# Per-image products of the diffuser as six pairs of heads on four column or row groups

## The reference

```python
k = (ref @ k_w).reshape(NB_REF, N, HEADS, hd).transpose(0, 2, 1, 3)
for _ in range(STEPS):                                    # 3
    qv = (x @ qv_w).reshape(B, N, 2, HEADS, hd).transpose(2, 0, 3, 1, 4)
    q, v = (qv[0], qv[1])
    attn = jnp.einsum('bhnd,rhmd->brhnm', q, k) * scale   # 12 heads of 16
    attn = jnp.einsum('brhnm,brhkm->brhnk', attn, attn)
    o = jnp.einsum('brhnk,bhkd->brhnd', attn, v)
    o = o.reshape(B, NB_REF, N, C)    # head-major, without a transpose back
    x = jnp.mean(o.transpose(0, 2, 3, 1), axis=-1)
    x = _layernorm(x @ proj_w + proj_b, ln_g, ln_b)
```

## Time and profile before

| | |
|---|---|
| median of three runs | 565.02 us (564.35 to 565.89) |
| the profiled execution | 566.11 us, its span 564.3 us |
| mean granted clock of TensorE | 0.804 of 2.4 GHz |
| busy: PE, PEld, DVE, ACT, POOL | 442.6, 365.1, 295.7, 244.8, 209.2 us |

### The profile page before, as it was taken

One profiled execution on the slowest core, in us unless ns is written; L12 is line 12 of the kernel. 1 busy time (PEld: TensorE's weight loads), 2 busy tenths in 40 slices (PEclk: granted clock), 3 DMA queues, 4 the chain that ended last, 5 costly groups with the idle time before them and its releaser, 6 DMA issues.

```text
span 564.3 us, 12817 instructions
## 1 busy us (share of the span) xinstructions
PE 442.6 (78%) x4112; PEld 365.1 (65%) x4112; DVE 295.7 (52%) x914; ACT 244.8 (43%) x724; POOL 209.2 (37%) x318
## 2 busy tenths in 40 slices
PE   3992699799999973789999997731989898989800
PEld 3972567587888752779998986631866666666600
DVE  0110423255555668687789775455545454545456
ACT  0130235566666641477656763111544444444300
POOL 1000004355455558353656552453232323232233
PEclk9996579799999975576767675555799999999955
DMA  8709525364455530000000000012111111100041
GB/s 263 202 23 322 163 46 122 77 161 94 100 116 117 112 82 0 1 2 2 2 2 14 25 14 14 18 47 90 51 37 33 32 34 36 32 15 19 6 145 44
DMA packets 52031, 38.32 MB, mean 68 GB/s; under 512 B 36059, under 2 KB 45445, under 8 KB 51200
## 3 DMA queue, kind: packets, MB, share of 16 engines
q1 hardware_dynamic: 48704, 26.78, 18.9%
q10 hardware_dynamic: 1008, 7.15, 3.9%
q0 software_dynamic: 2256, 3.57, 2.0%
HBM read 23.89 MB, written 14.33 MB: 68 GB/s over the span
## 4 chain that ended last, share of the span: by engine, by line
PE 68%; DVE 9%; issue 7%; POOL 4%; DMA 4%; ACT 3%; ACTq 3%; SPq 1%; POOLq 0%; DVEq 0%
PE bank L337 61%; PE bank L342 3%; PE bank L509 3%; ACTq L648 2%; ACT xT L738 2%; DVE h L1118 2%; POOL srt_dram L1174 1%; DMA bdm<-in_bdm 1%; PE bank L585 1%; DVE stats L815 1%; POOL rstd L1147 1%; DMA xT<-in_w 1%; SPq L274 1%; DVE xT L823 0%; ACT xT L633 0%
## 5 line engine op out<-in xcount | busy, mean ns | idle before, releaser
L337 PE MATMUL bank<-xh,w1h 96*128 96x128 f16 x300 | 69.6, 233 | 13.1 <-issue 11.9
L337 PE MATMUL bank<-xT 108*108 108x17 f16 (+5 forms) x904 | 67.9, 255 | 15.2 <-ACT xT L633 10.9
L337 PE MATMUL bank<-xl,w1h 96*128 96x128 bf16 x300 | 67.3, 225 | 0.0
L337 PE MATMUL bank<-xh,w1l 96*128 96x128 f16 x300 | 67.1, 224 | 0.0
L337 PEld LDWEIGHTS bank<-xT 108*108 108x108 bf16 (+4 forms) x904 | 50.9, 162 | 22.8 <-ACT xT L633 11.0
L791 ACT ACTIVATE xT<-bank,b 128x128 f32<-128x128 f32 x150 | 47.0, 364 | 41.3 <-PE bank L337 41.0
L633 ACT ACTIVATE xT<-bank 108x192 f32<-108x192 f32 (+3 forms) x117 | 40.1, 397 | 55.4 <-PE bank L337 37.5
L1217 POOL DMA_INDIRECT y_dram<-qkbm,ydst x25 | 24.8, 991 | 96.5 <-DVE qkbm L1109 87.5
L337 PEld LDWEIGHTS bank<-xh,w1h 96*128 x300 | 29.7, 99 | 32.8 <-issue 19.3
L666 ACT ACTIVATE xT<-bank,gains 96x128 f32<-96x128 f32 (+1 forms) x72 | 28.8, 457 | 40.8 <-PE bank L585 32.5
L1146 POOL TENSOR_SCALAR veps<-mv 108x1 f32<-108x1 f32 (+1 forms) x57 | 14.1, 248 | 84.9 <-DVE mv L817 84.3
(11 more groups left out here) (191 smaller groups left out, 1108.1 us busy)
## 6 DMA issues: line engine op xcount, KB each, us to landing
srt_dram<-row ACTq DMA_DIRECT2D x8, 800.2 KB, 10.4
xT<-in_xT SPq DMA_DIRECT2D x11, 324.0 KB, 7.1
xT<-srt_dram SPq DMA_DIRECT2D x25, 97.0 KB, 1.9
hT<-in_w SPq DMA_DIRECT2D x8, 288.0 KB, 3.3
xT<-in_w SPq DMA_DIRECT2D x8, 288.0 KB, 3.0
xT<-in_w SPq DMA_DIRECT2D x4, 576.0 KB, 3.9
hT<-in_w SPq DMA_DIRECT2D x4, 576.0 KB, 4.0
scratch<-xT SPq DMA_DIRECT2D x72, 27.0 KB
```

The costliest lines, as they stand in the source:

```text
L337: return nc.tensor.matmul(o, l, r, start=start, stop=stop)
```

## The change

R and o are cut into pairs of heads (PAIR = 32 features, GB = 6 pairs). R: six products, each with 32 stationary columns of qp and 3 x 32 = 96 moving columns of vm, written to the partitions 32 (g mod 4) of bank 3, so that the products lie on four column groups of the array. o: six products, each with 32 contraction rows at partition 32 (g mod 4) of q^T and rm, so on four row groups, with 96 columns out: the three images side by side. Nothing is summed over images any more; of the 3 x 192 columns of each token the right third is picked when the tile is stored, by the DMA's source. q^T is plain (qTb, two copies, 128 and 64 features), vm is one VectorE instruction, and osb is three times as wide, with three buffers (OB). o needs four banks, so the transposes of oc move to the second half of bank 0 and the projection into bank 1 beside q^T. The order within a turn changes on TensorE, ScalarE and VectorE: tile i + 1 of xs is transposed a turn ahead, the projection stands between R and o, and VectorE centres before it masks R. The mask colm (121.5 KB) gives way to pairm (16 KB).

```diff
+PAIR = 2 * HD
+GB = C // PAIR
+OB = 3
...
+        wide = ctx.enter_context(nc.psum_tensor("wide", [128, 4, 512], F32))
+        bank += [wide[:, r] for r in range(4)]
...
-                                     osb[j * N:(j + 1) * N, i % 4].rearrange("p (h d) -> p h d", h=HEADS)
+                                     osb[j * N:(j + 1) * N, i % OB, j].rearrange("p (h d) -> p h d", h=HEADS)
...
 # TensorE
+            def to_features(i):
+                pe.wait_ge(S["xs_ready"], i + 1)
+                if i >= 1:
+                    pe.wait_ge(S["xT_ready"], i)
+                if i >= 7:
+                    pe.wait_ge(S["ocT_ready"], i - 6)
+                turn(halves(0), xs[:, i % MT]).then_inc(S["xT_psum"], 1)
+            to_features(0)
             for i in range(NI + 5):
+                q, p = i - 1, i - 5
+                if p >= 0:
+                    pe.wait_ge(oc_loaded[p % 4], 16 * (p // 4 + 1))
+                    pe.wait_ge(S["xT_ready"], min(i + 1, NI))
+                    if p >= 1:
+                        pe.wait_ge(S["ocT_ready"], p)
+                    turn(halves2, oc[:, p % 4]).then_inc(S["ocT_psum"], 1)
+                if i + 1 < NI:
+                    to_features(i + 1)
                 if i < NI:
+                    pe.wait_ge(S["xT_ready"], i + 1)
+                    if i >= 1:
+                        pe.wait_ge(S["qT_ready"], i)
+                    if p >= 1:
+                        pe.wait_ge(S["y_read"], p)
+                    for u in range(2):
+                        cols = slice(u * P, min(C, (u + 1) * P))
+                        for k in range(2):
+                            last = mm(bank[1][0:cols.stop - cols.start, u * T:(u + 1) * T], wq[:, k, cols], xTs[:, i % 2, k, :], k == 0, k == 1)
+                    last.then_inc(S["qT_psum"], 1)
+                    if i >= 1:
+                        pe.wait_ge(S["qp_ready"], i)
+                        pe.wait_ge(S["vm_ready"], i)
                     for k in range(2):
                         last = mm(bank[2][0:T, 0:2 * C], xTs[:, i % 2, k, :], wqv[:, k, :], k == 0, k == 1)
                     last.then_inc(S["qv_psum"], 1)
+                if 0 <= q < NI:
                     pe.wait_ge(S["qp_ready"], q + 1)
                     pe.wait_ge(S["vm_ready"], q + 1)
                     if q >= 1:
                         pe.wait_ge(S["rm_ready"], q)
-                    for f in range(2):
-                        last = mm(bank[3 + f][0:HF, 0:JB * HF], qp[:, q % 2, f * HF:(f + 1) * HF], vm[:, q % 2, f].rearrange("p j c -> p (j c)"))
+                    for g in range(GB):
+                        rows, cols = slice(g % 4 * PAIR, (g % 4 + 1) * PAIR), slice(g * PAIR, (g + 1) * PAIR)
+                        last = mm(bank[3][rows, g // 4 * JB * PAIR:(g // 4 + 1) * JB * PAIR], qp[:, q % 2, cols], vm[:, q % 2, :, cols])
                     last.then_inc(S["r_psum"], 1)
+                if p >= 0:
                     pe.wait_ge(S["ocT_ready"], p + 1)
+                    pe.wait_ge(S["qT_ready"], min(i + 1, NI))
                     if p >= 1:
                         pe.wait_ge(S["y_read"], p)
                     for k in range(2):
-                        last = mm(bank[7][0:T, 0:C], ocT[:, k, :], wpa[:, k, :], k == 0, k == 1)
+                        last = mm(bank[1][0:T, 2 * T:2 * T + C], ocT[:, k, :], wpa[:, k, :], k == 0, k == 1)
                     last.then_inc(S["y_psum"], 1)
+                if 0 <= q < NI:
+                    pe.wait_ge(S["rm_ready"], q + 1)
+                    pe.wait_ge(S["qT_ready"], q + 1)
+                    if q >= 1:
+                        pe.wait_ge(S["o_ready"], q)
-                    for f in range(2):
-                        for j in range(JB):
-                            last = mm(bank[5][0:T, f * HF:(f + 1) * HF], qTm[:, q % 2, f, j, :], rm[:, f, j, :], j == 0, j == JB - 1)
+                    for g in range(GB):
+                        rows, u = slice(g % 4 * PAIR, (g % 4 + 1) * PAIR), g // 4
+                        last = mm(bank[4 + g % 4][0:T, u * JB * PAIR:(u + 1) * JB * PAIR], qTb[rows, q % 2, u], rm[rows, q % 2, u].rearrange("p j c -> p (j c)"))
                     last.then_inc(S["o_psum"], 1)
...
 # ScalarE, turn i: ocT of tile p, xTs of tile i + 1 (from_turn), h, the weight piece, qp, osb
-                    for j in range(JB):
-                        last = nc.scalar.activation(vm[:, i % 2, :, j, :], bank[2][0:T, C:2 * C].rearrange("p (f c) -> p f c", f=2), ACT.Copy, scale=rowm[:, j:j + 1])
-                    if q >= 4:
-                        act.wait_ge(oc_loaded[q % 4], 16 * (q // 4))
-                    copy(osb[:, q % 4], bank[5][0:T, 0:C]).then_inc(S["o_ready"], 1)
+                    if q >= OB:
+                        act.wait_ge(oc_loaded[(q - OB) % 4], 16 * ((q - OB) // 4 + 1))
+                    o = osb[:, q % OB].rearrange("p j (g c) -> p g j c", g=GB)
+                    for u in range(2):
+                        n = min(4, GB - 4 * u)
+                        last = copy(o[:, 4 * u:4 * u + n], wide[0:T, 0:n, u * JB * PAIR:(u + 1) * JB * PAIR].rearrange("p g (j c) -> p g j c", j=JB))
+                    last.then_inc(S["o_ready"], 1)
...
 # VectorE, turn i: qTb of tile i, centring of tile i - 6, rm of tile q, yb of tile p, vm of tile i, moments of tile p
+                    V.tensor_copy(qTb[0:P, i % 2, 0], bank[1][0:P, 0:T])
+                    V.tensor_copy(qTb[0:C - P, i % 2, 1], bank[1][0:C - P, T:2 * T]).then_inc(S["qT_ready"], 1)
...
+                    for u in range(2):
+                        rows = P if u == 0 else C - P
+                        last = V.tensor_tensor(rm[0:rows, q % 2, u], bank[3][0:rows, u * JB * PAIR:(u + 1) * JB * PAIR].rearrange("p (j c) -> p j c", j=JB),
+                                               pairm[0:rows, None, :].broadcast_to([rows, JB, PAIR]), ALU.mult)
+                    last.then_inc(S["rm_ready"], 1)
...
+                    dve.wait_ge(S["qp_ready"], i + 1)
+                    V.tensor_tensor(vm[:, i % 2], bank[2][0:T, C:2 * C][:, None, :].broadcast_to([T, JB, C]),
+                                    rowm[:, 0:JB, None].broadcast_to([T, JB, C]), ALU.mult).then_inc(S["vm_ready"], 1)
```

More of the change, by code:

```diff
@@ L58, in sem @@
             return ctx.enter_context(nc.semaphore(name))
[L60 removed]
+        bank = [ctx.enter_context(nc.psum_tensor(f"bank{i}", [128, 512], F32)) for i in range(4)]
+        wide = ctx.enter_context(nc.psum_tensor("wide", [128, 4, 512], F32))
+        bank += [wide[:, r] for r in range(4)]
         xT = sb("xT", [128, NT, KF, T])
@@ L87, in vit_kernel @@
         sel = sb("sel", [T, 2, T])
-        colm = sb("colm", [HF, JB, T])
+        pairm = sb("pairm", [P, PAIR])
         rowm = sb("rowm", [T, 4])
@@ L894, in _ @@
                         dve.wait_ge(S["o_psum"], i - 1)
-                    for f in range(2):
-                        last = V.tensor_tensor(qTm[:, i % 2, f], bank[1][0:HF, f * T:(f + 1) * T][:, None, :].broadcast_to([HF, JB, T]), colm[:], ALU.mult)
-                    last.then_inc(S["qTm_ready"], 1)
+                    V.tensor_copy(qTb[0:P, i % 2, 0], bank[1][0:P, 0:T])
+                    V.tensor_copy(qTb[0:C - P, i % 2, 1], bank[1][0:C - P, T:2 * T]).then_inc(S["qT_ready"], 1)
                 if i == 2:
@@ L1277 @@
         "ident": np.eye(P), "sel": sel,
-        "colm": np.broadcast_to((image[None] == np.arange(JB)[:, None])[None], (HF, JB, T)),
+        "pairm": (np.arange(P)[:, None] // HD % 2 == np.arange(PAIR)[None] // HD) * 1.0,
         "rowm": np.stack([image == 0, image == 1, image == 2, np.arange(T) >= FIRST_REF], 1),
```

139 lines of the change are left out of this document (57 added, 82 removed).

## The result

| | before | after |
|---|---|---|
| median of the runs | 564.68 us (561.37 to 565.89, 4 runs) | 638.9 us (631.48 to 644.07, 4 runs) |
| ratio | | 1.128, 95% interval 1.117 to 1.139 |
| profiled execution, span | 566.11, 564.3 us | 644.07, 642.3 us |
| steady turn | 5.17 us | 8.77 us |
| granted clock, mean over the profiled span | 0.80 | 0.67 |

The forecast was 549 us, with 0.10 for slower. The profiled execution of the changed kernel took longest of its four (the others 631.48 to 639.7 us at a mean clock of 0.68 to 0.69), so the spans differ by 78.0 us and the medians by 74.2.

What follows compares the result with a forecast made beforehand. TensorE, never waiting in the steady loop, was taken as the bound. Gains 13.1 + 1.8 + 1.7 + 0.7 - 0.3 - 0.7 = 16.3 us took 566.11 to 549.8; the median lies 1.09 lower, so 549, range 543 to 561.

Steps and rivals of the forecast that it cites:

- Groups run side by side in fp32: TensorE's r and o: products on different groups overlap, r 0.37 us for 0.97, o 0.38 for 1.13.
- the 16-bit row: Trace of another stage: 36 row-group products of 108 columns in 0.68 us, 0.013 each; fp32 assumed to behave alike.
- Rivals A and B: A: no groups overlap in fp32, 579 us, chance 0.06. B: only column groups serialize, 562 to about 570, chance 0.10.
- its upper end: For r with its weights in the open, rival B's slower case: a turn of 5.43 us, about 570 us in total.
- Four switches: Array mode goes full, column groups, full, row groups, full each turn; 4 x 0.09 = 0.36 us.
- the 0.50 of the sum: Per turn: 0.36 us for four switches, 0.05 for wpa's first weights, 0.09 for o's first weights.
- A turn of 4.40: TensorE's steady turn falls from 5.17 to 4.40 us; gain 0.77 x 17 = 13.1 us.
- Each term at the full clock: Steady-loop durations were read with TensorE at 2.4 GHz; only the cold start was taken as mostly at 1.2 GHz.
- VectorE and ScalarE: Work per turn extrapolated from durations by shape: VectorE 3.2 us, ScalarE at most 3.3, both fitting within 4.40.
- The margins: Spare time at hand-overs: rm to o 0.2 us, vm about 0.6, yb about 0.4, square root about 0.8 before rm.
- The gap and the tail: Gap at 92 to 112 us, waiting for weight pieces: 0.7 us gained. Tail: 0.7 us lost, bounds -2 and +2.
- The early turns: Three turns without reloads fall from 4.61 to 4.00 us each, gaining 1.8 us.

Runs made afterwards that it cites:

- c_wq_full: The changed kernel with wq's second product on 128 features instead of 64, so four mode changes a turn instead of six; 630.6 us.
- w_after_warm: The changed kernel with 14 whole-array products issued just ahead of the loop, so that it enters at the full clock; 638.1 us.
- p_wqv_x3: The changed kernel with wq's second product 128 wide and the whole-array wqv product issued three times over; 613.9 us.
- a_row_only: The changed kernel with r back as two whole-array products, wq in halves of 96, o on three row groups; 574.1 us.
- j: The kernel before with six tiny row-group products added in each turn, making twelve mode changes; 767.9 us.
- k_adjacent: The changed kernel with wq's second product 128 wide and o one turn later, right behind r, three mode changes a turn; 632.0 us.
- g: The kernel before with three tiny row-group products added in each turn, making six mode changes; 624.1 us.

## Why the prediction was wrong

- *Groups run side by side in fp32.* Right, for rows as the 16-bit row said and for columns, for which there was no row. Rivals A and B did not happen. The rule that the prediction quoted from the Trainium skill ("TensorE: Matmul & The Clock Gate", Part 3), that weight loads overlap only where the row group differs, would have put r at its upper end; the trace does not agree (r takes 0.47 at the full clock, for 1.01 one after the other).
- *Four switches.* Mis-sized. There are six, since wq's 64 outputs are a mode of their own (c_wq_full, with them 128 wide, has a turn 0.29 shorter at half clock). The 0.09 for one was right at the full clock, but late first weights come with five of the six (0.04 to 0.09 each by the single records, 0.34 in all), not with wpa and o alone: together 0.90 for the 0.50 of the sum. The Trainium skill ("TensorEngine Tiling (Array Packing)", Tiling Modes) lists 128x64 as a configuration and says that changing the mode drains the engine; read beside the diff it gives the six, and the trace agrees that each costs time.
- *A turn of 4.40.* By starts at the full clock (w_after_warm; r, wpa and the second pair of transposes from p_wqv_x3), measured for forecast: transposes 0.41 for 0.38, wq 1.06 for 0.82, wqv with its drain 1.47 for 1.38, r 0.47 for 0.51, wpa 0.83 for 0.84, o 0.56 for 0.47: 4.80 for 4.40, and 0.24 of the 0.40 is wq with the two changes around its 64 outputs. The half-clock turn agrees: with 6 x 0.125 that does not scale, 8.77 = 2x + 0.75 gives x = 4.01 and 4.76 at the full clock. 0.4 x 17 is 6.8 us, so some 556 would have been right had all else held. That 8.77 is also twice 4.39 is a coincidence.
- *Each term at the full clock.* This is the step that failed, and the prediction never wrote it down. Every duration in the sum was read at the earlier trace rows's 1.00 and none of the rivals asked whether the new mixture of products would still be granted it. The 17 turns cost 8.77 - 4.80 = 3.97 us more each for it, 67 us. The rest of the 78.0: 6 us less for the turn of 4.80 in place of 5.17, and 17 us more in the stretches on both sides, most of which ran at half clock for longer too.
- *VectorE and ScalarE.* rm 0.41 (0.39 forecast), vm 0.75 (0.77), osb 0.71 (0.75): the extrapolations held. The margins that rested on them did not: where the turn ran at the full clock (a_row_only) rm was late by 0.26 to 0.87 us, because of the centring ahead of it. I took 0.36 for that, which is what it takes in the loop of the kernel before, where it did not run beside GpSimd; over the changed kernel's 17 turns its mean is 0.72.
- *The gap and the tail.* The early turns cost 6.1 us for six turns of which each is some 3 us longer: the gap for the weight pieces took the rest.

What stays open is why the clock is not granted. Shown are: a loop with the kernel before's products does not get it when twelve changes are put in (j); the changed kernel's loop does not win it back after a warm start (w); added whole-array work brings it back with four changes in place (p). Cleared are the order, half-filled groups, the number or the rate of changes taken alone (k_adjacent against g), and the amount of row-group or of column-group work taken alone. Not cleared: that r's column groups together with o's row groups in one turn do it. Every kernel with both stayed low except p, and no run here takes the changes away and leaves both.

## What to carry to other kernels

A sum of durations read at one clock holds only if the changed stretch keeps that clock; ask it of every change that cuts whole-array products into groups, and look at the granted clock before any wait. Count for each change between array modes, at the full clock, a drain of 0.09 us ahead of it and up to 0.09 for late weights behind it, an output of 64 columns among wider ones being two. Of the kernels here all with two changes in a turn had the full clock in their steady turns; of those with three to six and both kinds of group only p did. And where a queue is reordered on an engine that GpSimd can hold up, take the longest duration of the moved instruction beside it, not that of a free one.

## What the runs showed of the hardware

- TensorE records that touch each other for 148.78 us (260.00 in j_before_6tokens) went with a granted clock of 0.50 throughout: a busy engine in the profile is not an engine at full clock.
- fp32 products on four column groups and on four row groups run at the same time, two more products in idle groups for nothing (a turn of 8.44 us with and without). The drain at a change of mode took 0.09 to 0.10 us at 2.4 GHz and 0.14 at 1.2.
- Added work made a kernel faster: 613.9 us with the wqv product three times, 630.6 with it once.
- VectorE's 0.36 us instruction took 2.53 us beside GpSimd's 2.37 and 1.80 beside its 1.64.
